# Expert routing by group, and the first two experts in passes by group

## The chip, the cores and the metric

The kernel runs on one core of one Trainium2 chip. The metric is the device time of one execution in microseconds. Before the change it is 599.27 us, the median of 3 runs (598.54 to 599.59).

## What is computed

The input is `x`, 16 batches of 128 rows of 256 float32 numbers (2048 tokens), and a context of the same shape. Four residual layers follow each other, each on the layer norm of `x`: a gated linear attention, a feed-forward layer with quantised weights and activations, a 16-head attention, and a mixture of experts. The change touches the last one, whose core in the reference is

```python
router_probs = jax.nn.softmax(router_logits, axis=-1)
gate, idx = jax.lax.top_k(router_probs, K)                 # K = 2 of 8 experts
mask_kt = jnp.swapaxes(mask, 1, 2).reshape(G, K * T, E)
pos = jnp.cumsum(mask_kt, axis=1) * mask_kt - 1.0          # place in the expert, within the group
disp_k = jax.nn.one_hot(pos, C, dtype=jnp.float32) * mask[..., None]
expert_in = jnp.einsum('gtec,gth->egch', dispatch, x)
h = jax.nn.relu(jnp.einsum('egch,ehf->egcf', expert_in, wi))
expert_out = jnp.einsum('egcf,efh->egch', h, wo)
y = jnp.einsum('gtec,egch->gth', combine, expert_out)
```

The tokens form G = 2 groups of T = 1024 (batches 0 to 7, and 8 to 15). Each expert takes at most C = 160 tokens of a group: 320 places in all. The place of a token depends on the tokens ahead of it in its own group only.

## The kernel before

The work is tiled by batch, 128 rows at a time ("tile" 0 to 15). The order on every engine is written out by hand, in one Python block per engine, and engines wait for each other on named semaphores (`pe.wait_ge(s["h_relu"], n)`). PE does the matmuls, VectorE (`dve`) and ScalarE (`act`) evacuate PSUM and do the elementwise work, POOL issues indirect DMAs (gathers and scatters of rows by index), SyncE (`sp`) the plain ones.

The end of the attention. VectorE and ScalarE normalise the tiles into `XR` (`norm4`, `norm4_act`); PE turns them two tiles at a time (`d_turn(p)`), ScalarE keeps the turned ones in `KT` (`xt4(p)`). PE computes the router's logits: tiles 0 to 7 in `d_logits`, 8 to 11 in `d_logits4`, both turned back by `d_back` and `d_back4`, and 12 to 15 by `d_row`. SyncE stores `XR` to the DRAM buffer `token_rows`, 4 tiles in a DMA.

The routing (L1386 to L1436, VectorE). When the logits of all tiles are there, the two largest of 8 are found for every token, one-hot in `OHs`; a scan gives the sums over tiles (`cum`); PE counts with two matmuls (L1989, L1991); `place` is each token's place in each expert. The softmax goes to `LG` and is stored as 8 more columns of each row in `token_rows`.

From places to token numbers, once for each expert e: `select(e)` (L1442) makes 16 one-hot matrices of 128 x 192 in `SEL`, one for each tile (for e = 0 ScalarE makes the last four, L871). PE multiplies them with the token numbers, split in two digits (`e_tokens`, L2004), VectorE keeps the result (`digits`, L1449), PE adds the digits up (`e_places`, L2013 to L2015), VectorE writes `token` (L1452). The 320 places are three chunks: chunk 0 and chunk 1 are the first 128 places of group 0 and of group 1, chunk 2 the last 32 places of both (64).

An expert. POOL gathers the three chunks of rows from `token_rows` into `XE` (`rows_in`, L511); VectorE takes the gate's column out (`gcol`, L1463); PE turns the rows (`e_turn`, L2041), ScalarE keeps them (`xet`, L888). `e_hidden`: 8 tiles of hidden units, each 2 float32 matmuls of 320 columns (L2057; a float32 matmul is two instructions in the trace), and a relu on ScalarE after each (`relu`, L895). `e_out`: chunk 2 (L2068), then chunk 0 (L2075), then the transposes of the next expert's rows, then chunk 1 (L2075). POOL gathers the running sums of the same tokens from `out` into `YG`, VectorE adds gate times result (`add_rows`, L1470 to L1478), POOL scatters the rows back (L513). The sums of an expert are gathered only after the scatter of the expert before has landed. The token and place matmuls of expert e + 1 stand inside `e_hidden(e)`, at hidden tiles 1 and 3 (4 and 6 for e = 0).

SyncE loads the 1 MB `wi` and `wo` of expert e + 2 as soon as expert e has left its buffer:

```python
free_after(sp, s["h_done"], e, NFT)     # wi: behind the last hidden matmul of e - 2
free_after(sp, s["ec_done"], e, 3)      # wo: behind the last output chunk of e - 2
```

Ahead of the rows of expert 0 PE runs dummy matmuls (`keep_busy`, L1498), 13 + 4 + 2 of them, two instructions each.

Of the kernel before, what the change touches and what calls it, by code (L numbers as in the profile page):

```python
# [7 lines left out]
BF16 = mybir.dt.bfloat16  # L8
# [77 lines left out]
def build(nc, A, out):  # L86
# [22 lines left out]
    with ctx:  # L109
# [218 lines left out]
        SEL_DVE = 12  # L328
# [16 lines left out]
        def _(sp):  # L345
# [38 lines left out]
            def weights_in(e, u, h):  # L384
                if isinstance(e, int) and e < 2:
                    sp.wait_ge(s["u_again"], len(LATE))
                free_after(sp, s["h_done"], e, NFT)
                sp.dma_start(WI[:, u], A["L1_ffn_wi"][bass.ds(e, 1)].squeeze(0).rearrange("(k p) f -> p k f", p=P)).then_inc(s[f"wi_in{u}"], 16)

            def weights_out(e, u, h):  # L390
                free_after(sp, s["ec_done"], e, 3)
                sp.dma_start(WO[:, u], A["L1_ffn_wo"][bass.ds(e, 1)].squeeze(0).rearrange("(k p) f -> p k f", p=P)).then_inc(s[f"wo_in{u}"], 16)
            weights_in(0, 0, 0)
            weights_out(0, 0, 0)
            weights_in(1, 1, 0)
            weights_out(1, 1, 0)

# [4 lines left out]
            xr = xr_d.rearrange("(b p) d -> p b d", p=P)  # L402
            for q in range(XQ):

                if q == 1:
                    sp.wait_ge(s["xr_act"], 4)
                else:
                    sp.wait_ge(s["xr_ready"], (2, 0, 4, 6)[q])
                sp.dma_start(xr[:, 4 * q:4 * q + 4, 0:D], XR[:, 4 * q:4 * q + 4, 0:D]).then_inc(s["xr_out"], 16)
            sp.wait_ge(s["probs"], 1)  # L410
            sp.dma_start(xr[:, :, D:], LG[:, :, :]).then_inc(s["xr_out"], 16)

            def both(e, u, h):
                if isinstance(e, int) and e < 2:
                    return
                weights_in(e, u, h)
                weights_out(e, u, h)
            steps(sp, NE, [(both, 0)])
# [5 lines left out]
        def _(pool):  # L424
# [77 lines left out]
            pool.wait_ge(s["xr_ready"], 6)  # L502
# [4 lines left out]
            def indirect(e, c, dram, sbuf, gather):  # L507
                n = P if c < 2 else ROWS - 2 * P
                where = bass.IndirectOffsetOnAxis(ap=token[0:n, e, c:c + 1], axis=0)
                if gather:  # L510
                    return nc.gpsimd.indirect_dma_start(out=sbuf[0:n, c, :], out_offset=None, in_=dram, in_offset=where,  # L511
                                                        bounds_check=NB * S - 1, oob_is_err=False)
                return nc.gpsimd.indirect_dma_start(out=dram, out_offset=where, in_=sbuf[0:n, c, :], in_offset=None,  # L513
                                                    bounds_check=NB * S - 1, oob_is_err=False)
            pool.wait_ge(s["xr_out"], 16 * (XQ + 1))
            pool.wait_ge(s["x3_out"], 16 * XQ)
            def rows_in(e):
                pool.wait_ge(s["token_ready"], e + 1)
                if e >= 2:
                    pool.wait_ge(s["xe_tr"], e - 1)  # L520
                    pool.wait_ge(s["gcol_ready"], e - 1)
                for c in range(3):

                    indirect(e, c, xr_d, XE[:, e % 2], True).then_inc(s[f"xe_in{e % 2}" if e or c == 2 else f"xe_first{c}"], 16)
            rows_in(0)
            for e in range(NE):
                if e + 1 < NE:
                    rows_in(e + 1)
                if e >= 1:
                    pool.wait_ge(s["rows_out"], 16 * 3 * e)  # L530
                for c in range(3):
                    indirect(e, c, out_rows, YG, True).then_inc(s["yg_in"], 16)
                for n, c in enumerate((2, 0, 1)):
                    pool.wait_ge(s["y_ready"], 3 * e + n + 1)
                    indirect(e, c, out_rows, YG, False).then_inc(s["rows_out"], 16)
# [3 lines left out]
        def _(act):  # L539
# [257 lines left out]
            def lt4_copy():  # L797
                act.wait_ge(s["d_lg"], 2)
                nc.scalar.activation(XCT[:, 1, 0, :], ps[7][:, 0:P], ACT.Copy).then_inc(s["d_lt"], 1)
# [54 lines left out]
            xt4(0)  # L854
            xt4(1)
# [1250 lines left out]
```

## Time and profile before

| | |
|---|---|
| median of 3 runs | 599.27 us |
| the profiled execution | 599.31 us, its span 597.6 us |
| PE busy | 515.6 us (86% of the span) |
| VectorE, ScalarE, POOL busy | 375.3, 321.8, 141.2 us |
| first hidden matmul of expert 0 | 431.67 us |
| first hidden matmul of expert 2 | 472.47 us |
| moved by DMA | 37.58 MB |

All times in what follows count from the start of the span, in the one profiled execution; the time of a run is the span and 1.7 us around it. A row of a timeline gives start, duration, engine, line, what was written from what, the shapes, a count where rows are merged, and in brackets how long the engine was idle before and what ended that. The chain of waits is the path that ended last, followed back from the end.

### The profile page before, as it was taken

To read this page: it belongs to the slowest core of one execution; us is meant where nothing else is said; L and a number is where in the kernel's file an instruction comes from. 1 tells how busy PE (TensorE), PEld (TensorE's weight loads), DVE (VectorE), ACT (ScalarE), POOL (GpSimd) and SP (SyncE) were. 2 spreads that over 40 slices of the span, in tenths; PEclk is the share of its full clock that TensorE was granted. 3 is DMA by queue.
4 is the path that set the end of the run, shared out by engine and by line. 5 is a ranking of instruction groups with operands and counts; after the bars stand their busy time and mean duration, and the time that the engine had idled before them with its cause. 6 is when DMAs were issued, how large, how long until landed. Compare 5 with 4: busy or idle time off the path is not lost.

```text
span 597.6 us, 9312 instructions
## 1 busy us (share of the span) xinstructions
PE 515.6 (86%) x3284; PEld 364.1 (61%) x3284; DVE 375.3 (63%) x944; ACT 321.8 (54%) x672; POOL 141.2 (24%) x202
## 2 busy tenths in 40 slices
PE   1979989899999700899989999996799999999994
PEld 1558846654444300787657787874667776777773
DVE  6576689845489989779678699987403332143101
ACT  1836658723389969771298899984222112211220
POOL 2005635000000000000323133111234344434431
PEclk9979999999999955999999999999699999999998
DMA  7910000000000000025000101015133536353410
GB/s 213 274 53 1 2 2 1 2 1 0 0 0 1 0 1 1 0 102 181 2 0 2 36 3 37 1 38 176 28 110 120 185 120 204 118 183 120 133 44 22
DMA packets 31994, 37.58 MB, mean 63 GB/s; under 512 B 8656, under 2 KB 27728, under 8 KB 31952
## 3 DMA queue, kind: packets, MB, share of 16 engines
q1 hardware_dynamic: 28880, 29.07, 14.8%
q0 software_dynamic: 3072, 7.95, 4.6%
q8 instruction: 26, 0.43, 0.3%
q14 instruction: 16, 0.13, 0.1%
HBM read 30.14 MB, written 6.88 MB: 62 GB/s over the span
## 4 chain that ended last, share of the span: by engine, by line
PE 71%; DVE 14%; ACT 8%; issue 2%; SPq 2%; DMA 1%; POOL 1%; POOLq 0%; DVEq 0%
PE pA L2057 12%; PE pB L2075 9%; PE pC L1726 6%; PE pC L1765 5%; PE pA L1759 3%; PE pB L1775 3%; PE pA L1681 2%; PE pC L1587 2%; PE pC L1681 2%; PE pB L1681 2%; PE pC L2068 2%; DVE am L1180 2%; PE pC L1633 2%; PE pB L1855 2%; DVE arena L1176 2%
## 5 line engine op out<-in xcount | busy, mean ns | idle before, releaser
L477 POOL TENSOR_TENSOR arena<-KT,par 128x256 f32<-128x256 f32 x32 | 19.0, 614 | 248.0 <-DVE XIT L1254 186.0
L2057 PE MATMUL pA<-arena 128*128 128x320 f32 x256 | 74.1, 438 | 0.4 <-ACT arena L883 0.4
L895 ACT ACTIVATE arena<-pA 128x320 f32<-128x320 f32 x64 | 28.0, 437 | 71.8 <-PE pA L2057 71.8
L2075 PE MATMUL pB<-arena 128*128 128x256 f32 x256 | 59.3, 385 | 0.0
L2057 PEld LDWEIGHTS pA<-arena 128*128 128x128 f32 x256 | 47.4, 190 | 18.9 <-issue 1.1
L2075 PEld LDWEIGHTS pB<-arena 128*128 128x128 f32 x256 | 47.4, 190 | 9.4 <-issue 3.1
L1146 DVE TENSOR_REDUCE am<-arena 128x1 f32<-128x512 f32 x48 | 32.1, 681 | 23.0 <-ACT arena L647 22.9
L1726 PE MATMUL pC<-wdnT,XIT 128*128 128x256 f32 x192 | 42.9, 381 | 1.8 <-DVE XIT L1254 1.8
L1330 DVE TENSOR_REDUCE rm<-pA 128x16 f32<-128x2048 f32 x16 | 36.7, 2291 | 8.8 <-PE pA L1759 8.8
L1726 PEld LDWEIGHTS pC<-wdnT,XIT 128*128 128x128 f32 x192 | 36.0, 190 | 7.9 <-DVE XIT L1254 2.8
L1765 PE MATMUL pC<-ident,arena 128*128 128x128 f32 x240 | 35.4, 280 | 1.5 <-ACT XIT L743 0.8
L513 POOL DMA_INDIRECT out<-arena,token x24 | 23.5, 977 | 55.1 <-DVE arena L1478 45.7
L780 ACT ACTIVATE arena<-pC 128x512 f32<-128x512 f32 x60 | 34.9, 605 | 0.9 <-PE pC L1765 0.9
L511 POOL DMA_INDIRECT arena<-token_rows,token x24 | 24.2, 1010 | 44.3 <-DVE token L1452 26.2
L1463 DVE COPY gcol<-arena 128x3 f32<-128x3 f32 x8 | 1.4, 174 | 52.8 <-DMA arena<-token_rows,token 52.8
L1765 PEld LDWEIGHTS pC<-ident,arena 128*128 128x128 f32 x240 | 26.1, 141 | 10.4 <-ACT arena L767 4.6
L1498 PE MATMUL pB<-ident 128*128 128x128 f32 x64 | 12.5, 372 | 21.7 <-DVE arena L1227 21.7
L1339 DVE TENSOR_TENSOR arena<-pA,rm 128x1024 f32<-128x1024 f32 (+1 forms) x32 | 29.1, 952 | 0.5
L888 ACT ACTIVATE arena<-pA 128x320 f32<-128x320 f32 x14 | 5.4, 435 | 43.8 <-PE pA L2041 43.8
L767 ACT ACTIVATE arena<-arena 128x1024 f32<-128x1024 f32 (+1 forms) x32 | 28.1, 881 | 0.0
L511 POOL DMA_INDIRECT arena<-out,token x24 | 23.7, 988 | 9.2 <-issue 7.0
L1498 PEld LDWEIGHTS pB<-ident 128*128 128x128 f32 x64 | 11.7, 280 | 21.8 <-issue 21.7
(341 smaller groups left out, 1152.7 us busy)
## 6 DMA issues: line engine op xcount, KB each, us to landing
arena<-in_L_ffn_wi SPq DMA_DIRECT2D x8, 1024.0 KB, 5.3
arena<-in_L_ffn_wo SPq DMA_DIRECT2D x8, 1024.0 KB, 5.8
X<-in_x SPq DMA_DIRECT2D x4, 512.0 KB, 6.3
arena<-in_ctx SPq DMA_DIRECT2D x4, 512.0 KB, 7.8
out<-X SPq DMA_DIRECT2D x4, 512.0 KB, 2.9
token_rows<-arena SPq DMA_DIRECT2D x4, 512.0 KB, 5.4
arena<-in_L_ffn_w_up SPq DMA_DIRECT2D x1, 768.0 KB, 7.8
arena<-in_L_ffn_w_gate SPq DMA_DIRECT2D x1, 768.0 KB, 9.7
```

The lines of the kernel that those rows point to most:

```text
L511: return nc.gpsimd.indirect_dma_start(out=sbuf[0:n, c, :], out_offset=None, in_=dram, in_offset=where, bounds_check=NB * S - 1, oob_is_err ...
L767: nc.scalar.activation(part, part, ACT.Exp).then_inc(s["p_ready"], 1)
L780: nc.scalar.activation(PT[:, u, 4 * g:4 * g + 4, :], bank.rearrange("p (k n) -> p k n", k=4), ACT.Copy).then_inc(s["pt_ready"], 1)
L895: nc.scalar.activation(HT[:, u, f, :], ps[2 + f % 2][:, 0:ROWS], ACT.Relu).then_inc(s["h_relu"], 1)
L1146: V_.tensor_reduce(am[:, 0 if name == "gate" else 1, cols(c * FT + f, 1)], t[:, f, cols(c, 512)], AX.X, ALU.max, apply_absolute_value=True ...
L1330: V_.tensor_reduce(rm[:, u, :], sco, AX.X, ALU.max, negate=True).then_inc(s["rm_ready"], 1)
L1339: V_.tensor_tensor(PR[:, u, part], sco[:, part], rm[:, u, part].unsqueeze(2).broadcast_to([P, part.stop - part.start, P]), ALU.add).then_i ...
L1681: last = mm(ps[2 + f][:, :], w[:, k, f * P:(f + 1) * P], XITv[:, k, cols(c, 512)], start=(k == 0), stop=(k == KD - 1))
L1726: last = mm(ps[6 + u][:, 0:D], OT[:, u, f, :], wdnT[:, f, :], start=(f == 0), stop=(f == FT - 1))
L1765: last = tr(bank[:, n * P:(n + 1) * P], PR[:, u, 4 * g + n, :], ident[:, :])
L2057: last = mm(ps[2 + f % 2][:, 0:ROWS], WI[:, u, k, f * P:(f + 1) * P], XET[:, u, k, :], start=(k == 0), stop=(k == KD - 1))
L2075: last = mm(ps[4 + c][:, 0:D], HT[:, u, f, c * P:(c + 1) * P], WO[:, u, f, :], start=(f == 0), stop=(f == NFT - 1))
```

## The change

Everything of the routing that depends on one group is done for that group alone. Group 0 goes first, as soon as the logits of tiles 0 to 7 are there. Expert 0 and expert 1 are done in two passes each, in the order (0, A), (1, A), (0, B), (1, B): pass A is chunk 0 (128 places, all of group 0), pass B the other 192 places. Experts 2 to 7 are one pass "F" each, as before. The routing of group 1 stands on VectorE between the steps of passes 0 and 1.

```diff
-        SEL_DVE = 12
+        PASSES = [(0, "A"), (1, "A"), (0, "B"), (1, "B")] + [(e, "F") for e in range(2, NE)]
+        CHUNKS = {"A": (0,), "B": (2, 1), "F": (2, 0, 1)}
+        GROUPS = {"A": (0,), "B": (1,), "F": (0, 1)}
```

SyncE: the rows and probabilities of each group have a semaphore of their own, and `wi` and `wo` wait for the passes:

```diff
+            def normed_out(q):
+
+                if q % 2:
+                    sp.wait_ge(s["xr_act"], 2 * q + 2)
+                else:
+                    sp.wait_ge(s["xr_ready"], q + 2)
+                sp.dma_start(xr[:, 4 * q:4 * q + 4, 0:D], XR[:, 4 * q:4 * q + 4, 0:D]).then_inc(s[f"xr_out{q // 2}"], 16)
...
             for q in range(XQ):
...
+                normed_out(q)
+            probs_out(0)
+            probs_out(1)
+            for e in range(2, NE):
+                weights_in(e, e % 2)
+                weights_out(e, e % 2)
```

POOL: the gathers of the A passes start when group 0 is in `token_rows`:

```diff
+            pool.wait_ge(s["xr_out0"], 16 * 3)
+            rows_in(0)
+            rows_in(1)
             pool.wait_ge(s["x3_out"], 16 * XQ)
...
+            sums_in(0)
+            pool.wait_ge(s["xr_out1"], 16 * 3)
+            rows_in(2)
+            sums_out(0)
+            rows_in(3)
+            for i in range(1, len(PASSES)):
+                if 3 <= i < len(PASSES) - 1:
+                    rows_in(i + 1)
+                sums_in(i)
+                sums_out(i)
```

ScalarE: the turned tiles 0 to 3 are kept ahead of the last `at_copy`, the logits' copy goes ahead of the last inverse square root, and the normalisation of tiles 12 to 15 comes from VectorE. The four selections on ScalarE are gone (VectorE makes them).

```diff
             at_copy(NB - 2, 1 - u)
+            xt4(0)
+            xt4(1)
             at_copy(NB - 1, u)
...
             xt4(3)
+            lt_copy()
             rsqrt(8, 4, 12)
             xt4(4)
             xt4(5)
-            lt_copy()
             lt4_copy()
+            act.wait_ge(s["xr_ready"], 5)
+            for b in range(12, NB):
+                norm4_act(b)
+            exp4(0)
             xt4(6)
             xt4(7)
...
+            exp4(1)
```

VectorE: the same steps as before, for one group of 8 tiles at a time:

```diff
+            logits_0()
+            largest(0)
+            less_largest(0)
+            link(choose(0, 0))
+            chosen_off(0)
+            second(0)
+            tile_sums(0)
+            probabilities(0)
+            find_places(0)
+            select(0, 0)
+            logits_1()
+            digits_kept(0)
+            largest(1)
+            less_largest(1)
+            number(0)
+
+            select(1, 0)
+            link(choose(1, 0))
+            chosen_off(1)
+            digits_kept(1)
+            second(1)
+            number(1)
+            tile_sums(1)
+            probabilities(1)
+            find_places(1)
+            select(0, 1)
+            gate_column(0)
+            digits_kept(2)
+            select(1, 1)
+            number(2)
+            add_rows(0)
+            digits_kept(3)
+            gate_column(1)
+            number(3)
+            for i in range(2, len(PASSES)):
+                if i >= 4:
+                    digits_kept(i)
+                    number(i)
+                gate_column(i)
+                if i == 2 or 4 <= i < len(PASSES) - 1:
+                    for g in range(NG):
+                        select(2 if i == 2 else i - 1, g)
+                add_rows(i - 1)
+            add_rows(len(PASSES) - 1)
```

PE: the places inside the passes, and the start. The transposes of the next pass stand ahead of the last full chunk, in an A pass inside its only chunk:

```diff
+            def e_hidden(i):
...
+                    if i == 0 and f == 2:
+                        count(1)
+                    if i == 1 and f == 2:
+                        e_tokens(3)
+                    if i == 1 and f == 5:
+                        e_places(3)
+                    if 3 <= i < len(PASSES) - 1 and f == 1:
+                        e_tokens(i + 1)
+                    if 3 <= i < len(PASSES) - 1 and f == 3:
+                        e_places(i + 1)
...
+                for c in full:
+                    if c == full[-1] and part != "A" and i + 1 < len(PASSES):
+
+                        e_turn(i + 1)
+                    for f in range(NFT):
+                        if part == "A":
+                            if i == 0 and f == 1:
+                                e_tokens(2)
+                            if (i, f) in ((0, 4), (1, 6)):
+                                e_turn(i + 1)
+                            if i == 0 and f == 5:
+                                e_places(2)
...
             d_turn(6)
-            d_back()
-            d_back4()
             d_turn(7)
+            count(0)
             for b in range(12, NB):
                 d_row(b)
...
             e_tokens(0)
             e_places(0)
-            e_turn(0, 0, 0)
-            flat(NE, [(e_hidden, 0), (e_out, 0)])
+            keep_busy(ps[4], 8)
+            e_tokens(1)
+            e_places(1)
+            keep_busy(ps[4], 8)
+            e_turn(0)
+            for i in range(len(PASSES)):
+                e_hidden(i)
+                e_out(i)
```

The order of the indirect DMAs on POOL, from the first one on. Before (`token_rows` are gathers of rows, `out` as a source gathers of sums, `out` as a target scatters; each row is a chunk, or as many as its count says):

```order
L511 DMA arena<-token_rows,token 128x264 x2
L511 DMA arena<-token_rows,token 64x264
L511 DMA arena<-token_rows,token 128x264 x2
L511 DMA arena<-token_rows,token 64x264
L511 DMA arena<-out,token 128x256 x2
L511 DMA arena<-out,token 64x256
L513 DMA out<-arena,token 2048x256 x3
```

and now:

```order
L530 DMA arena<-token_rows,token 128x264 x2
L530 DMA arena<-out,token 128x256
L530 DMA arena<-token_rows,token 128x264
L530 DMA arena<-token_rows,token 64x264
L532 DMA out<-arena,token 2048x256
L530 DMA arena<-token_rows,token 128x264
L530 DMA arena<-token_rows,token 64x264
L530 DMA arena<-out,token 128x256
L532 DMA out<-arena,token 2048x256
L530 DMA arena<-out,token 128x256
L530 DMA arena<-out,token 64x256
L532 DMA out<-arena,token 2048x256 x2
```

One chunk of rows, not three, stands ahead of the first pass; the next three rows of expert 2 (L530, `token_rows`) follow behind the last row shown, the two scatters of pass 2.

PE at the end of an expert and the start of the next, before:

```order
L2068 MATMUL pC<-arena 64x256 x8
L2075 MATMUL pB<-arena 128x256 x8
L2041 MATMUL pA<-ident,arena 128x128 x2
L2041 MATMUL pA<-ident,arena 128x64
L2041 MATMUL pA<-ident,arena 128x128 x2
L2041 MATMUL pA<-ident,arena 128x64
L2075 MATMUL pB<-arena 128x256 x8
L2057 MATMUL pA<-arena 128x320 x2
```

and now, at the end of pass 3 (expert 1, B), ahead of expert 2:

```order
L2141 MATMUL pA<-arena 128x192 x10
L2155 MATMUL pC<-arena 64x256 x8
L2118 MATMUL pA<-ident,arena 128x128 x2
L2118 MATMUL pA<-ident,arena 128x64
L2118 MATMUL pA<-ident,arena 128x128 x2
L2118 MATMUL pA<-ident,arena 128x64
L2171 MATMUL pB<-arena 128x256 x8
L2141 MATMUL pA<-arena 128x320 x2
```

One full chunk of 8 matmuls less stands between the hidden part and the transposes of expert 2's rows.

## Rows read from the trace of the kernel before

**Rows 1.** The page: granted clock of TensorE in 40 slices, and the weight loads of the hidden matmuls.
```profile
PEclk9979999999999955999999999999699999999998
...
L2057 PEld LDWEIGHTS pA<-arena 128*128 128x128 f32 x256 | 47.4, 190 | 18.9 <-issue 1.1
```

**Rows 2.** Windows: span, its length, busy us and count of each engine, granted clock, DMA.
```profile
410.00:420.00 10.00, 2.94 (x22) 2.27 (x20) 7.73 (x30) 2.15 (x7) 1.33 (x2) 0.78 0.42 116
420.00:430.00 10.00, 8.49 (x55) 7.53 (x56) 1.77 (x9) 1.76 (x5) 3.23 (x3) 0.54 0.16 37
```

**Rows 3.** The chain of waits, 395 to 600 us: start, us, what.
```profile
423.27 5.84 PE pB L1498 x26
429.11 0.37 PE pA L2025 x2
429.48 0.89 PE pB L1498 x8
...
431.67 4.57 PE pA L2057 x16
...
442.85 4.90 DMA arena<-token_rows,token
...
462.30 1.88 PE pC L2068 x16
464.18 3.65 PE pB L2075 x16
467.82 0.99 PE pA L2041 x6
...
472.47 1.08 PE pA L2057 x4
473.55 0.44 PE pC L2004 x16
...
571.50 8.61 PE pA L2057 x32
```

**Rows 4.** Timeline of VectorE, 397 to 500 us: start, us, instructions, idle before.
```profile
407.00 0.16 DVE L927 TENSOR_TENSOR s<-yv 128x4 f32<-128x4 f32 x1 [0.67 <-ACT yv L546]
...
409.90 0.23 DVE L1390 COPY XIT<-pB 128x64 f32<-128x64 f32 x1 [0.73 <-PE pB L1899]
...
412.26 0.19 DVE L1397 COPY XIT<-pC 128x32 f32<-128x32 f32 x1 [1.48 <-PE pC L1909]
...
418.76 2.24 DVE L1442 TENSOR_SCALAR arena<-cidx,XIT 128x192 bf16<-128x192 bf16 x12
422.25 0.56 DVE L1449 CAST XIT<-pC 128x384 bf16<-128x384 f32 x1 [1.25 <-PE pC L2004]
423.31 0.22 DVE L1452 TENSOR_SCALAR token<-pC 128x2 uint32<-128x2 f32 x2 [0.50 <-PE pC L2015]
...
463.02 0.20 DVE L1463 COPY gcol<-arena 128x3 f32<-128x3 f32 x1 [6.05 <-DMA arena<-token_rows,token]
...
468.44 0.43 DVE L1470 COPY arena<-pC 64x256 f32<-64x256 f32 x1 [2.36 <-DMA arena<-out,token]
```

**Rows 5.** Timeline of ScalarE, 397 to 432 us: the normalisation of two tiles.
```profile
399.78 1.12 ACT L791 ACTIVATE arena<-X,s,rstd 128x256 f32<-128x256 f32 x2
```

**Rows 6.** Timeline of POOL, 425 to 500 us, and of SyncE's queue: DMA issues.
```profile
424.54 1.27 POOL L511 DMA_INDIRECT arena<-token_rows,token  x1 [13.21 <-issue]
...
440.25 1.00 POOL L511 DMA_INDIRECT arena<-token_rows,token  x1 [11.86 <-DVE token L1452]
...
457.79 1.05 POOL L511 DMA_INDIRECT arena<-token_rows,token  x1 [1.13 <-DVE token L1452]
...
464.32 0.97 POOL L511 DMA_INDIRECT arena<-out,token  x1 [0.30 <-issue]
...
441.76 0.39 SPq L388 DMA_DIRECT2D arena<-in_L_ffn_wi  x1
```

**Rows 7.** The chain of waits, 46 to 60 us: matmuls of 128 float32 columns.
```profile
51.80 1.98 PE pC L1587 x16
```

More of the change, by code:

```diff
@@ L516, in _, with rows_in @@
-            pool.wait_ge(s["x3_out"], 16 * XQ)
[L517 to L535, printed above, removed]
+            def rows_in(i):
+                e, part = PASSES[i]
+                pool.wait_ge(s["token_ready"], i + 1)
+                if part == "F":
+                    pool.wait_ge(s["xe_tr"], i - 1)
+                    pool.wait_ge(s["gcol_ready"], i - 1)
+                for c in sorted(CHUNKS[part]):
+                    indirect(e, c, xr_d[0:TG * S, :] if part == "A" else xr_d, XE[:, e % 2], True, (TG if part == "A" else NB) * S).then_inc(s[arrived(i)[0]], 16)
@@ L896, in _, with relu @@
-            steps(act, NE, [(xet, 0), (relu, 0)])
+            def relu(i):
+                e, part = PASSES[i]
+                if part == "F":
+                    act.wait_ge(s["ec_done"], PIECES[i - 1])
+                n = places(part)
+                for f in range(NFT):
+                    act.wait_ge(s["h_done"], i * NFT + f + 1)
+                    nc.scalar.activation(HT[:, e % 2, f, n], ps[2 + f % 2][:, 0:n.stop - n.start], ACT.Relu).then_inc(s["h_relu"], 1)
+            for i in range(len(PASSES)):
+                xet(i)
+                relu(i)
@@ new lines, in select, with digits_kept @@
+            def select(e, g):
+                if e >= 2 and g == 0:
+                    dve.wait_ge(s["id_done"], e + 1)
+                for b in range(g * TG, (g + 1) * TG):
+                    last = V_.tensor_scalar(SEL[:, e % 2, b, :], cidx[:, g, :], place[:, g, e, b % TG:b % TG + 1], None, ALU.is_equal)
+                last.then_inc(s["sel_ready"], 1)
+            def digits_kept(i):
+                e, part = PASSES[i]
+                n = slice(SELW * GROUPS[part][0], SELW * (GROUPS[part][-1] + 1))
+                dve.wait_ge(s["id_done"], i + 1)
+                V_.tensor_copy(digits[:, e % 2, n], ps[7][:, n]).then_inc(s["id_kept"], 1)
@@ new lines, in e_tokens @@
+            def e_tokens(i):
+                e, part = PASSES[i]
+                if i >= 1:
+                    pe.wait_ge(s["token_ready"], i)
+                for g in GROUPS[part]:
+                    pe.wait_ge(s["sel_ready"], i + 1 if i < 4 else 2 * e + g + 1)
+                    for b in range(g * TG, (g + 1) * TG):
+                        o = 32 * (b % 4)
+                        last = mm(ps[7][o:o + 32, g * SELW:(g + 1) * SELW], ids[:, 2 * b:2 * b + 32], SEL[:, e % 2, b, :],
+                                  start=(b % TG < 4), stop=(b % TG >= 4))
+                last.then_inc(s["id_done"], 1)
@@ new lines, in e_turn @@
+            def e_turn(i):
+                e, part = PASSES[i]
+                u = e % 2
+                name, n = arrived(i)
+                pe.wait_ge(s[name], n)
+                if i >= 1:
+                    pe.wait_ge(s["xet_ready"], i)
+                for k in range(KD):
+                    for c in sorted(CHUNKS[part]):
+                        n = P if c < 2 else SHORT
+                        if part == "A":
+                            last = tr(ps[u][:, k * P:(k + 1) * P], XE[:, u, 0, k * P:(k + 1) * P], ident[:, :])
+                        else:
+                            o = c * P - places(part).start
+                            last = tr(ps[k][:, o:o + n], XE[0:n, u, c, k * P:(k + 1) * P], ident[0:n, 0:n])
+                last.then_inc(s["xe_tr"], 1)
```

402 lines of the change are left out of this document (176 added, 226 removed).

## The prediction

> **What bounds the kernel now.** I first read the page: the TensorE clock is full in most slices, but two stretches and a few single slices stand below [rows 1]. The diff touches only the end of attention and the expert stage, so I then read the windows around 400 to 480 us. From 410 to 420 us PE works 2.9 of 10 us, and from 420 to 430 us it works 8.5 us at a granted clock of 0.54 [rows 2]. The chain of waits says what that work is: 5.84 us of 26 dummy matmuls (L1498) that only keep the array busy until the rows of expert 0 arrive, and the first useful expert matmul is at 431.67 us [rows 3]. From there PE is the chain: an expert costs 19.8 us, 8.6 of them hidden matmuls (L2057), 1.88 the short chunk (L2068), 3.65 each full chunk (L2075), 0.99 the transposes, 0.44 the token matmuls of the next expert (L2004). So two things set the end: when the experts start, and how long PE takes from there. Between 412 and 424 us the chain is VectorE, one small instruction after another [rows 4].
>
> **The change, part by part.** Times are absolute, in the profiled execution (span 597.6 us, 599.31 us in all; the median of the runs is 599.27, so the two agree).
>
> *Group 0 is routed first.* Before, the whole routing starts when the last logits are there, at 412.26 us, and ends with the tokens at 423.31 + 0.22 = 423.53 [rows 4]. Now the chain of group 0 needs only tiles 0 to 7. I follow it: four evacuated transposes, the logits, their copy and the transpose back end near 408.35 us; VectorE then still has its inverse square root, which waits for ScalarE as before (407.00, [rows 4]), but behind the 0.6 us copy of the logits that now goes ahead of it, so about 409.0. Four normalisations that stood ahead of the logits copy went to ScalarE, 0.56 each [rows 5], 2.2 us beside VectorE's chain. The logits take 0.5 us. The 17 linked steps to the places are 64 wide instead of 128. A 64-wide copy takes 0.23 [rows 4], a step with its issue 0.26 to 0.28, so 4.7 us. Eight selections cost 8 x 2.24/12 = 1.5 us; then come logits of group 1 (0.4), the digits at half width (0.35 instead of 0.56), two steps of group 1 (0.5), and the places and the number (0.2). That gives tokens at 417.2 us, **6.3 us earlier**.
>
> *One gather instead of three ahead of the first matmul.* Before it was 431.67 - 423.53 = 8.1 us. Now: POOL starts its DMA 1.0 us after the tokens, and the first gather was down 429.11 - 424.54 = 4.6 us later, by the transposes that follow it [rows 3, 6]; then come 4 transposes' instructions (0.11 each, from L1498 at full clock, 8 in 0.89 [rows 3]), 0.2 of drain and one 0.4 us copy: 6.5 us, **1.6 us less**. The dummy matmuls (two blocks of 16 instructions, 1.8 us each at full clock) are hidden by that landing if the clock stays up. First expert matmul: 423.7 us, **8.0 us earlier**.
>
> *Two experts become four passes.* Before, experts 0 and 1 take 472.47 - 431.67 = 40.8 us [rows 3]. The columns are the same, but narrow matmuls are not as cheap as their width. For 128 columns the trace has a row of the same kind, L1587: 16 instructions in 1.98 us, 0.124 each [rows 7], where 320 columns cost 8.61/32 = 0.269 [rows 3]. Each hidden tile of pass A has 4 of them, 0.50 us, and must wait for the relu of two tiles before: 0.50 + some 0.35 of drain and signals + 0.28 for the relu make 1.13 us per two tiles, 4.5 us in all. In pass B, 192 columns give 0.16 each, 5.3 us.
> Pass 0: 4.5 + 0.2 (counting of group 1) + 3.65 + 0.2 (tokens) + 0.45 (transposes) + 0.1 (places) = 9.1. Pass 1: 4.5 + 0.3 + 3.65 + 0.65 = 9.1. Pass 2: 5.3 + 1.9 + 0.65 + 3.65 = 11.5. Pass 3: 5.3 + 0.45 + 0.2 + 0.45 (waits for the digits, which stand behind the additions of pass 2 on VectorE) + 1.9 + 1.0 + 3.65 = 12.95. Sum 42.65: **1.85 us more**, without waits for rows.
> The bounds of the unknown price of 128 columns: 0.107, the width alone scaled from 320 columns, and 0.190, the duration of a weight load of L2057 [rows 1], if loads can't overlap. L1587 loads 128x128 float32 weights too and repeats at 0.124, so I take that. The Trainium skill ("TensorE: Matmul & The Clock Gate", LDWEIGHTS) says that a load takes columns / 1.2 ns whatever the matmul's width; its 107 ns for 128 columns would make a pass A's hidden part 3.4 us at best. This is no end of my range.
>
> *A new wait, at the end of pass 3.* Expert 2's rows are transposed after the short chunk and **one** full chunk before (5.5 us after the hidden part); in pass 3 the order is short chunk, transposes, full chunk, so only 1.9 us after. Let T be the start of pass 3's hidden part. PE wants the rows at T + 6.4 + 1.9 = T + 8.3. POOL has queued ahead of them the two stores of pass 2, and those wait for the additions, which wait for sums gathered at about T - 5 and T - 3.7 (sums land 4.1 us after the last issue, 464.32 to 468.44 in the steady stage [rows 4, 6]); so the additions end at T + 2.2, the stores at T + 4.8, and the three gathers start at T + 5.1. A quiet gather of three takes 463.02 - 457.79 = 5.2 us [rows 4, 6]; but SP loads the 1 MB of `wi` of expert 3 when the hidden part ends, at T + 6.4, 1.3 us behind the first gather. Expert 1 of before has the same collision: gathers from 440.25, `wi` at 441.76, rows at 447.75, 7.5 us [rows 3, 6]. That is 7.5 us after the first gather and 6.0 after `wi`. So the rows come at T + 12.4 to 12.6, and PE waits **4.0 us** or a little more; quiet it is 2.0, and with the sums there in time and quiet, 1.0. I take 4.0, since the offset of `wi` is nearest to the row of expert 1.
> The Trainium skill ("DMA: Bandwidth & Descriptors", Anatomy of one DMA) gives a transfer issued by GpSimd 2.0 us fixed plus its bytes; by it the last gather would land about T + 11, and the wait would be 2.7. The rows of before, 5.2 and 7.5 for three, are above it.
>
> *What costs nothing.* Group 1's routing (some 7 us of VectorE up to 430 us) stands beside passes 0 and 1, 18 us in which VectorE has little else; if it slipped past them, pass 2 would wait for its rows, needed at about 440 and landed by about 438. The probabilities of group 0 are stored in a queue behind the last quarter of the rows, at 413.7, and are there by 417.1; POOL needs them at 418.2. The number of indirect DMAs stays 72, and the tail is the same.
>
> Sum: -8.0 + 1.85 + 4.0 = -2.15, so 599.31 - 2.15 = **597.2 us**.
>
> **The rivals.**
> 1. *Small collision.* The wait in pass 3 is 1.0 to 2.5 us: 594.2 to 595.7. For it: in the steady stage gathers land in 5.2 us. Against it: the load of `wi` begins beside them.
> 2. *The clock falls in the routing* (slower). Before, it fell after PE's work stopped at 412 us and came back only at 429 us, after the long dummy block, whose instructions took 0.225 each in it [rows 2, 3]. Now PE has short bursts in 410 to 422 us (transposes, logits, tokens, dummies) with gaps of 0.5 to 1.8 us. If these don't hold the clock, the single-tile logits (1.8 us more, 1.3 behind VectorE), the dummies (3.6 us per block, the second now ending after the rows are there) and the transposes bring the first expert matmul to about 427.2, 3.5 us later, and the hidden part may run slowly for up to 3 us, 1.5 more: 600.7 to 602.2. It decides wherever the clock falls between 410 and 422 us. Against it: no gap is as long as the one of before.
> 3. *Narrow matmuls are bound by weight loads of 0.19.* Hidden parts of 32 x 0.19 = 6.1 us in four passes: 2 x 1.6 + 2 x 0.8 = 4.8 more, and the wait in pass 3 gives nothing back, since it goes with T: 602.0. Against it stands L1587 at 0.124.
> 4. *The overlap is not reached*, since group 1's rows are late for pass 2. Every us there is one us; 2 us make 599.2.
>
> **How the numbers follow.** Forecast 0.5, small collision 0.17, clock 0.2, weight loads 0.04, late group 1 0.09. A measurement can tell about 0.2%, 1.2 us. The forecast itself has +-1.5 us from its steps, so a fifth of it lies within 1.2 us of no change; faster is 0.40 + 0.17 + 0.04 (half of late group 1) = 0.61, the same 0.10 + 0.04 = 0.14, slower 0.20 + 0.04 + 0.01 = 0.25. The range goes from the small collision with its lower bounds, 593.0 (the width alone at 128 columns takes another 1.0 off), into the clock's case, 601.0, and leaves out about 2 in 10.
>
> **What would show it.** In the profile after: first hidden matmul near 423.7 us; passes of 9, 9, 11.5 and 17 us; 32 hidden matmuls of 128 columns in about 4.5 us; a DMA wait of PE near 461 us of some 4 us in front of expert 2's transposes, and the experts from 2 on 19.8 us each. A granted clock of 0.5 between 412 and 425 us, or a wait ahead of pass 2, would prove it wrong.

## The result and the profile after

| | before | after |
|---|---|---|
| median | 599.17 us (598.52 to 599.59, 5 runs) | 602.48 us (601.61 to 603.18, 5 runs) |
| span of the profiled execution | 597.6 us | 600.6 us |
| first hidden matmul | 431.67 | 425.54 |
| first hidden matmul of expert 2 | 472.47 | 475.46 |
| mean granted clock over the span | 0.948 | 0.946 |

The ratio is 1.005, 95% interval 1.0039 to 1.0062: slower by half a per cent, outside the range given. The experts do start 6.1 us earlier, but the four passes to expert 2 take 9.1 us more than the two experts did.

The page's clock line of after (40 slices of 15.0 us) has two dips behind 400 us where the one of before has one [rows 1]: a 7 from 405 to 420 us, earlier than the 6 of before, and a new 7 from 465 to 480 us.
```profile
PEclk9979999999999955999999999997999799999998
```

The windows of after: length, busy us (count) of PE, PE weight load, VectorE, ScalarE, POOL, then granted clock, DMA share, GB/s. The first two answer to [rows 2].
```profile
410.00:420.00 10.00, 8.09 (x49) 7.11 (x46) 7.81 (x39) 3.72 (x9) 0.60 (x1) 0.63 0.40 119
420.00:430.00 10.00, 8.99 (x72) 7.88 (x70) 5.55 (x26) 2.36 (x9) 2.68 (x3) 0.86 0.23 45
460.00:470.00 10.00, 5.86 (x34) 3.77 (x33) 2.32 (x14) 1.39 (x6) 4.37 (x5) 0.86 0.57 180
470.00:480.00 10.00, 10.00 (x50) 7.36 (x50) 3.29 (x11) 1.71 (x5) 1.94 (x2) 0.80 0.34 108
```
From 410 to 420 us PE is busy for 8.1 us where it was busy for 2.9, and still the granted clock is 0.63, below the 0.78 of before. Part of the 8.1 us is the same work stretched by the half clock, so a busy share says little of how much work was done. In the trace the granted clock stands at 0.5 (the level of 1.2 GHz) from 412.6 to 422.8 us and from 467.2 to 474.0 us.

The chain of waits of after, at the start: start, us, what. It answers to [rows 3].
```profile
413.68 3.32 PE pC L1994 x16
417.00 0.47 PE pC L2088 x7
...
418.16 3.62 PE pB L1585 x16
421.78 0.47 PE pC L2088 x7
...
422.95 1.90 PE pB L1585 x16
424.84 0.23 PE pA L2115 x2
...
425.54 1.16 PE pA L2141 x8
...
426.80 3.12 PE pA L2141 x24
```
The clock can be read from the durations: the same block of 16 dummy instructions (L1585) took 3.62 us the first time and 1.90 the second, once ahead of the clock's return at 422.8 us and once behind it. The sixteen logits instructions of the last four tiles (L1994) took 3.32 us at half clock.

The timeline of VectorE of after (idle before and its releaser in brackets) shows who paid for that; it answers to [rows 4].
```profile
414.30 1.53 DVE L1488 TENSOR_SCALAR arena<-cidx,XIT 128x192 bf16<-128x192 bf16 x8
417.10 0.19 DVE L1436 COPY XIT<-pC 128x32 f32<-128x32 f32 x1 [1.27 <-PE pC L1994]
...
418.22 0.15 DVE L1501 TENSOR_SCALAR token<-pC 128x1 uint32<-128x1 f32 x1
```
VectorE was at the selections on time (414.30, forecast 414.2), then waited 1.27 us for logits that PE still had in hand. The tokens are there at 418.37 instead of the forecast 417.2.

The second place is the end of pass 3, in PE's timeline of after:
```profile
461.62 1.95 PE L2155 MATMUL pC<-arena 128*64 128x256 f32 x16
467.70 1.90 PE L2118 MATMUL pA<-ident,arena 128*128 128x128 f32 x6 [4.14 <-DMA arena<-token_rows,token]
469.53 5.93 PE L2171 MATMUL pB<-arena 128*128 128x256 f32 x16
475.29 1.24 PE L2141 MATMUL pA<-arena 128*128 128x320 f32 x4
```
The wait for expert 2's rows is 4.14 us. Behind it the six transposes take 1.90 us where [rows 3] have 0.99, and the full chunk 5.86 in the chain (5.93 here, with its drain) where [rows 3] have 3.65: 0.9 + 2.2 = 3.1 us that are no wait at all and stand in no idle column.

Why the rows were late shows in the queues of POOL and SyncE (SPq) of after:
```profile
458.08 1.01 POOL L532 DMA_INDIRECT out<-arena,token  x1 [0.30 <-issue]
459.40 1.03 POOL L530 DMA_INDIRECT arena<-token_rows,token  x1 [0.31 <-issue]
460.74 1.02 POOL L530 DMA_INDIRECT arena<-token_rows,token  x1 [0.30 <-issue]
462.07 0.95 POOL L530 DMA_INDIRECT arena<-token_rows,token  x1 [0.30 <-issue]
...
461.72 0.37 SPq L404 DMA_DIRECT2D arena<-in_L_ffn_wi  x1
```
The last gather was issued at 462.07, the load of `wi` at 461.72, and the rows were down at 467.66, 5.59 us after the issue. The chain of waits of after shows what stood in line before them:
```profile
441.15 2.80 DMA arena<-out,token
...
445.28 2.45 DMA out<-arena,token
...
449.86 4.74 DMA arena<-out,token
...
462.07 5.59 DMA arena<-token_rows,token
```
From 437.5 to 467.7 us this chain runs through POOL, the transfers and VectorE's additions, and not through PE: sums of pass 1, its store, sums of pass 2, its stores, and only then the rows of expert 2. PE does its passes beside that and then waits for its end. So the wait can be shortened by a faster transfer (e2 below) or by another order on POOL (e4).

### The profile page after: what moved, and what is told of

The parts are those of the page before. It is cut to its first block, busy times and chain, and to the rows that moved or that the text cites. A ratio compares the mean times of both kernels' runs of the same rounds, so it can differ in the third digit from the quotient of the medians.

```text
span 600.6 us, 9381 instructions
## 1 busy us (share of the span) xinstructions
PE 521.1 (87%) x3344; PEld 372.4 (62%) x3344; DVE 377.8 (63%) x968; ACT 323.5 (54%) x687; POOL 141.5 (24%) x202
## 4 chain that ended last, share of the span: by engine, by line
PE 69%; DVE 13%; ACT 8%; DMA 4%; issue 3%; POOL 1%; POOLq 0%; SPq 0%; DVEq 0%
PE pA L2141 10%; PE pB L2171 9%; PE pC L1813 6%; PE pC L1852 5%; PE pA L1846 3%; PE pB L1862 3%; PE pA L1768 2%; PE pC L1674 2%; PE pB L1768 2%; PE pC L1768 2%; DVE am L1217 2%; PE pC L1720 2%; PE pB L1942 2%; DVE arena L1213 2%; DVE am L1183 2%
## 5 line engine op out<-in xcount | busy, mean ns | idle before, releaser
L2141 PE MATMUL pA<-arena 128*128 128x320 f32 (+2 forms) x320 | 75.8, 387 | 0.5 <-ACT arena L916 0.5
L930 ACT ACTIVATE arena<-pA 128x320 f32<-128x320 f32 (+2 forms) x80 | 30.7, 384 | 75.6 <-PE pA L2141 75.6
L2141 PEld LDWEIGHTS pA<-arena 128*128 128x128 f32 x320 | 53.8, 190 | 15.9 <-issue 0.9
L2171 PE MATMUL pB<-arena 128*128 128x256 f32 x256 | 62.2, 396 | 0.0
L2171 PEld LDWEIGHTS pB<-arena 128*128 128x128 f32 x256 | 48.7, 196 | 9.3 <-issue 2.5
L530 POOL DMA_INDIRECT arena<-token_rows,token x24 | 24.4, 1015 | 44.4 <-DVE token L1501 25.3
L1585 PE MATMUL pB<-ident 128*128 128x128 f32 x58 | 10.7, 359 | 21.7 <-DVE arena L1264 21.7
L920 ACT ACTIVATE arena<-pA 128x320 f32<-128x320 f32 (+1 forms) x16 | 5.7, 408 | 43.6 <-PE pA L2118 43.6
L1511 DVE COPY gcol<-arena 128x3 f32<-128x3 f32 (+2 forms) x10 | 1.6, 164 | 40.1 <-DMA arena<-token_rows,token 40.1
L530 POOL DMA_INDIRECT arena<-out,token x24 | 23.8, 991 | 11.2 <-issue 6.7
L1521 DVE COPY arena<-pC 64x256 f32<-64x256 f32 x8 | 3.4, 426 | 33.7 <-DMA arena<-out,token 23.6
```

Of the source, the lines that this page charges most:

```text
L930: nc.scalar.activation(HT[:, e % 2, f, n], ps[2 + f % 2][:, 0:n.stop - n.start], ACT.Relu).then_inc(s["h_relu"], 1)
L2141: last = mm(ps[2 + f % 2][:, 0:n.stop - n.start], WI[:, u, k, f * P:(f + 1) * P], XET[:, u, k, n], start=(k == 0), stop=(k == KD - 1))
L2171: last = mm(ps[4 + c][:, 0:D], HT[:, u, f, c * P:(c + 1) * P], WO[:, u, f, :], start=(f == 0), stop=(f == NFT - 1))
```

## The experiments

Theory A: the prediction's three terms hold, and what it left out is the clock, which fell in the routing (1.8 us at the start) and again in the new wait (3.1 us behind it). Theory B: the pieces after the wait are slow for another reason (the transfers beside them, the split itself), and only a shorter chain helps. All ratios are to the kernel before on the same chip.

### Fill the wait (e1_warm_wait)

```diff
+                        if i == 3:
+                            pe.wait_ge(s["xet_ready"], 4)
+                            keep_busy(ps[0], 17)
                         e_turn(i + 1)
```

> The changed kernel (602.5 us) with 17 dummy matmuls (34 instructions, 0.11 us each, 3.8 us) ahead of the transposes of expert 2's rows, in the 4.1 us that PE waits there. Theory A: the wait itself costs 4.1 us, and the clock that falls in it another 3.1 us (transposes 1.9 for 1.0, the full chunk behind them 5.86 for 3.65). Then the wait stays, the clock stays at 1.00, and the time is 602.5 - 3.1 = 599.4. Theory B: the slow instructions behind the wait are slow for another reason (the 1 MB load beside them): 602.5, with the chunk at 5.9 us at a full clock.

Measured: 600.01 us (599.07 to 602.35, 10 runs), ratio 1.0022 (1.0008 to 1.0036); span 597.3, 3.3 less. PE's timeline, end of pass 3:
```profile
463.50 4.06 PE L1585 MATMUL pA<-ident 128*128 128x128 f32 x34
467.39 1.16 PE L2118 MATMUL pA<-ident,arena 128*128 128x128 f32 x6
468.48 3.72 PE L2174 MATMUL pB<-arena 128*128 128x256 f32 x16
```
The rows come only about half a us earlier (VectorE's copy of their gate column, which waits for them, starts at 467.13 instead of 467.68), but the transposes and the chunk run at full speed behind the dummies. Of the 3.3 us in the span 0.2 are an earlier first hidden matmul (425.30). This is the cleanest proof in the case: nothing was taken away, work of no use was added, and the kernel became 2.5 us faster in the medians, 1.7 by the two ratios (1.005 and 1.0022, whose intervals don't touch).

### Take the load out of the wait (e2_wi_late)

```diff
+                if e == 3:
+                    sp.wait_ge(s["xe_in0"], 16 * 5)
                 sp.dma_start(WI[:, u], A["L1_ffn_wi"][bass.ds(e, 1)]...
```

> The changed kernel with the load of wi of expert 3 held back on SyncE's queue until expert 2's rows have landed. Theory A: this load is what makes the three gathers take 8.3 us instead of the 5.2 of a quiet stage; rows at 459.4 + 5.2 = 464.6, PE wants them at 463.5, so a wait of 1.1 instead of 4.1, too short for the clock to fall: 602.5 - 3.0 - 3.1 = 596.4. Theory B: the gathers are late because of what is ahead of them on POOL or because of the stores of pass 2 that are still under way: landing stays at 467.7, 602.5.

Measured: 596.37 us (596.01 to 597.13, 4 runs), ratio 0.9956 (0.994 to 0.9973). POOL and SyncE:
```profile
461.63 0.95 POOL L532 DMA_INDIRECT arena<-token_rows,token  x1 [0.30 <-issue]
...
464.27 0.37 SPq L406 DMA_DIRECT2D arena<-in_L_ffn_wi  x1
```
the last gather's landing in the chain of waits:
```profile
461.63 2.33 DMA arena<-token_rows,token
```
and PE:
```profile
464.24 1.21 PE L2120 MATMUL pA<-ident,arena 128*128 128x128 f32 x6 [1.01 <-DMA arena<-token_rows,token]
465.38 3.72 PE L2173 MATMUL pB<-arena 128*128 128x256 f32 x16
```
With the 1 MB load behind it instead of beside it, the transposes can start 2.6 us after the last gather's issue instead of 5.6. The wait is 1.01 us, and no clock falls behind it. One wait on SyncE turns the change from slower into faster than before.

### Transposes later in the last chunk (e3_turn_late)

The transposes of expert 2's rows go behind six of the chunk's eight tiles in pass 3; the transfers are not touched.

> The changed kernel, with the transposes of expert 2's rows inside the last full chunk of pass 3, ahead of its 7th tile, not ahead of the chunk: PE wants the rows 2.75 us later, at 466.3, for a landing at 467.7. Theory A: a wait of 1.4 us, clock at 1.00: 602.5 - 2.7 - 3.1 = 596.7, if ScalarE's copy of the turned rows (0.8 us) hides behind the last two tiles. Theory B (clock or no clock, what stands behind is slow): 599.8.

Measured: 598.09 us (595.86 to 600.98, 10 runs), ratio 0.9978 (0.9958 to 0.9998). The wait was 1.23 us, and the granted clock from 460 to 480 us was 1.00, as expected. The median came out 1.4 us above the expectation; the profiled run stood 1.7 us late from before 402 us on, ahead of anything that was changed.

### Rows of expert 2 before the sums of pass 2 (e4_early_tokens)

The tokens of expert 2 are found in pass 2 (not 3), and POOL gathers its rows ahead of pass 2's sums and stores:

```diff
             for i in range(1, len(PASSES)):
-                if 3 <= i < len(PASSES) - 1:
+                if i == 2:
+                    rows_in(4)
+                if 4 <= i < len(PASSES) - 1:
                     rows_in(i + 1)
```

> The changed kernel, with the tokens of expert 2 found in pass 2 (not pass 3) and its rows gathered ahead of the sums of pass 2. Theory A: the rows are there by about 455, PE never waits for them: 602.5 - 4.1 - 3.1 = 595.3. The sums of pass 2 are gathered 2.6 us later, additions end at 459, ahead of the output of pass 3 at 461.6, so nothing is given back. Rival: POOL's queue is what bounds the stage, the additions of pass 2 come after 461.6 and PE waits for them instead: 597 to 599.

Measured: 596.60 us (595.42 to 597.09, 4 runs), ratio 0.995 (0.9933 to 0.9966). No wait is left in pass 3, and expert 2 starts at 470.08 instead of 475.46. At the start the clock was low for 13.7 us in this execution (10.2 in after), and the first hidden matmul was at 426.99: these 1.45 us are about the 1.3 that the expectation missed.

### Are the dummy blocks worth their time? (e6_no_dummies, e7_one_block)

On e4's order, `keep_busy(ps[4], 8)` is taken out at both places (e6), or replaced by one block of 12 just ahead of the transposes (e7).

> The kernel of e4 (596.6 us) without the two blocks of 8 dummy matmuls ahead of the first expert matmul. Theory A: the first hidden matmul is held back by the second block at half clock, not by the rows, which are there at about 424; without the blocks it comes at 424.8, but then passes 0 and 1 start at half clock, the hidden part of pass 0 takes 7 us for 4.3 and more behind it until the clock is back: 2 us earlier and 4 to 7 us slower, 598.5 to 601.5. Theory B: real matmuls bring the clock back as fast as dummies do, and the blocks are only in the way: 595.

> The kernel of e4 (596.6 us) without the first block of 8 dummies, and 12 instead of 8 in the second. At half clock the first block takes 3.6 us, in which the tokens of expert 1 wait behind it; without it the tokens of expert 1 come 1.7 us earlier and the one block of 24 instructions runs from about 421 to 426 at half clock, at best rising in between: the same first hidden matmul, 596.6 +- 0.8, if the clock rises after a stretch of full work of the same length; 595 if it rises earlier since the work is in one piece.

Measured: e6 596.34 us (595.87 to 597.5, 6 runs), ratio 0.9956 (0.9938 to 0.9973); e7 597.53 us (596.37 to 599.42, 12 runs), ratio 0.9972 (0.9959 to 0.9985). Neither is measurably apart from e4. PE's timeline of e6:
```profile
424.33 2.07 PE L2147 MATMUL pA<-arena 128*128 128x128 f32 x8 [0.47 <-ACT arena L918]
...
426.41 4.11 PE L2147 MATMUL pA<-arena 128*128 128x128 f32 x24
```
Without the blocks the first pass starts 2.7 us before e4's and runs its hidden part at half clock, 6.0 us instead of 4.3; with them the clock is back in time, but the second block, stretched to 3.7 us by the half clock, stands in the way. In the profiled executions e6 keeps 1.1 us of its lead (pass 2 begins at 444.05, in e4 at 445.18), in the medians 0.3 us are left, within the noise. Once the clock has fallen, dummies only buy back what they cost.

### Keep the clock from falling: dummies in the gaps (e5_warm_start, e8_warm_after)

```diff
             d_turn(5)
+            pe.wait_ge(s["x3_ready"], NB)
+            keep_busy(ps[5], 3)
             d_logits4()
+            keep_busy(ps[5], 2)
             d_back4()
+            keep_busy(ps[5], 3)
...
             d_turn(6)
+            keep_busy(ps[5], 1)
             d_turn(7)
```

The same lines on e4's order (e5) and on the changed kernel itself (e8).

> The kernel of e4 (596.6 us) with 9 dummy matmuls (18 instructions) in the gaps in which PE waits between 408.6 and 412.4 us, that is before the place at which the clock fell in all five profiles so far. Theory A: the clock falls because PE had too little to do in those gaps; filled, it stays at 1.00, the single-tile logits take 1.8 us for 3.5, the dummy blocks 1.8 for 3.6 and the first hidden matmul comes at 423.6, not 426.5 to 427.0: 596.6 - 3 = 593.6. Theory B: the clock falls anyway, because what PE does around 413 to 418 us is too thin too (8 columns per matmul), somewhat later: 595 to 597.

> The changed kernel itself (602.5 us) with the same dummies in the gaps between 408.6 and 412.4 us as e5. It tells the clock at the start from the wait in pass 3. Theory A: 1.9 us earlier start, the wait of 4.1 us and the clock that falls in it as before: 602.5 - 1.9 = 600.6, if the clock holds. Theory B: it falls all the same: 602.5.

Measured: e8 600.87 us (599.8 to 603.54, 12 runs), ratio 1.0031 (1.0016 to 1.0047): 1.6 us less than after in the medians (the intervals of the two ratios overlap), with the clock low for 3.4 us only and the first hidden matmul at 424.10; the wait in pass 3 and the fall behind it stayed. e5 602.08 us (599.33 to 605.33, 10 runs), ratio 1.0047 (1.0026 to 1.0068): 5.5 us slower than e4, against both expectations, though its start was 1.1 us earlier than e4's. Its chain of waits shows a new one:
```profile
460.44 1.00 POOL out L532
461.44 0.30 issue
461.75 5.85 DMA out<-arena,token
...
468.41 1.03 POOL arena L530
469.44 0.30 issue
469.75 5.05 DMA arena<-out,token
...
477.13 0.21 PE pC L2107 x2
```
and PE's timeline what it did:
```profile
470.19 2.42 PE L2151 MATMUL pA<-arena 128*128 128x320 f32 x8
477.13 0.21 PE L2107 MATMUL pC<-pick,XIT 128*128 128x1 bf16 x2 [4.52 <-DVE XIT L1497]
...
477.48 7.89 PE L2151 MATMUL pA<-arena 128*128 128x320 f32 x18
```
The load of `wi` was now issued at 462.10, 0.35 us behind the last store of pass 2 (461.75), and the store took 5.85 us, where a store of after with no load beside it (pass 1, 445.28) has 2.45 in the chain. The sums of pass 3 wait for that store, their additions stand on VectorE ahead of the digits of expert 3 (L1497), and PE waits for its places 4.52 us; then the clock falls again (18 hidden instructions in 7.89 us, 0.44 each, where 0.28 is usual). In e6, which has the same order, `wi` came 0.98 us after the store (461.32, 462.30), POOL could go on to the sums 3.3 us after that store's issue (6.7 in e5), and no such wait is there. That is no more than the 3.3 us of e9 below, where the load was held back, so 0.98 us between store and load were enough. The same load, at the same place of the program, hit another transfer.

### Hold the load again, then fill the start (e9, e10, e11)

e9 is e5 with the load of expert 3's `wi` held until the stores of pass 2 are down:

```diff
+                if e == 3:
+                    sp.wait_ge(s["rows_out"], 16 * PIECES[3])
```

e10 is e9 with one dummy behind each single-tile step, and e11 is e10 without the two blocks of 8:

```diff
             for b in range(12, NB):
                 d_row(b)
+                keep_busy(ps[4], 1)
```

> The kernel of e5_warm_start (early tokens, dummies in the gaps at the start), with one thing more: SyncE issues the wi load of expert 3 only when the stores of pass 2 have landed. Theory A (in e5 the load of 1 MB that was issued 0.35 us after those stores made them land 6.7 us after their issue, for 3.3 in e6, so that the sums of pass 3 were late, TensorE waited 4.5 us for the places of expert 3, and its clock fell): the stores land at about 465.1, no wait of over 1 us at 477, no low clock after 430, and a time of 595.5. Theory B (the stores were late by chance or by the gathers in front of them on their queue): the wait and the fall stay, 601 to 602. If the load itself comes too late for expert 3 (it needs it at about 477 and the load takes some 6 us from 465): no cost expected.

> e9_hold_wi with one dummy matmul more after each single-tile step of the router's transposes, so that TensorE is busy also where it did 8-column matmuls with waits between them. Theory A (the clock falls at the start because TensorE is idle for much of 408 to 420): the clock stays at 1.00 through the routing, the first hidden matmul starts at about 423.6 and at full pace, 593.2. Theory B (it falls in the long wait for the tokens, whatever is done before): low for some 10 us as in e5, 595.5.

> e10_warm_rows without the two blocks of 8 dummies ahead of the experts. If the blocks only delay the first hidden matmul (as e6 against e4 said), it starts some 1 us earlier than in e10 but at half clock if the clock falls without them: 594 to 595.5. If they hold the clock, this is 1 to 3 us slower than e10.

| | us | ratio | first hidden matmul |
|---|---|---|---|
| e9 | 594.96 (592.98 to 596.47, 6 runs) | 0.9922 (0.9898 to 0.9947) | 424.55 |
| e10 | 593.48 (593.08 to 595.07, 6 runs) | 0.9903 (0.9884 to 0.9922) | 423.33 |
| e11 | 594.78 (594.53 to 596.41, 6 runs) | 0.9924 (0.9905 to 0.9943) | 422.58, at half clock |

e9 against e5 shows that the collision was e5's loss: the sums are gathered at 463.37 and 464.71 instead of 468.41 and 469.75, the wait for the places is gone, and 7.1 us of the median with it. In the two profiled executions the difference is 8.9 us: 1.4 are the start, where the clock was low for 3.4 us in e9 and 10.2 in e5, in spite of the same program up to there, and 7.5 lie behind it.

The clock line of e10's page and its windows:
```profile
PEclk9979998999999955899999999999999999999998
...
410.00:420.00 10.00, 8.73 (x92) 7.46 (x83) 8.72 (x44) 3.72 (x9) 1.27 (x1) 1.00 0.42 126
420.00:430.00 10.00, 8.96 (x72) 7.80 (x73) 6.20 (x31) 2.61 (x9) 2.01 (x2) 1.00 0.23 45
```
e11, windows:
```profile
410.00:420.00 10.00, 6.87 (x68) 5.71 (x64) 8.73 (x43) 3.72 (x9) 1.27 (x1) 0.91 0.40 118
420.00:430.00 10.00, 8.29 (x47) 7.37 (x47) 4.51 (x22) 2.60 (x9) 2.00 (x2) 0.57 0.24 45
```
In the profiled execution of e10 the granted clock does not fall in the routing nor behind it (only the last slice, past the last matmuls, is below 9), and the first hidden matmul is at 423.33, which is where the prediction had put it (423.7). In e11 it falls where the blocks are missing, and the first pass's hidden part is slow again; that is 1.3 us in the medians and 1.7 in the spans. The two intervals overlap, but both kernels ran on the same chip, and five of the six executions of e10 are below all six of e11. So the blocks that were worth nothing in e4 are worth more than a microsecond here: they hold a clock, they don't bring it back for free.

### The change's own order, clock held at both places (e12_clock_held)

The changed kernel, with e8's dummies, the one behind each `d_row`, and e1's 17 in the wait.

> The changed kernel with its order of instructions kept, and only dummy matmuls added at both places where the clock fell: 9 in the gaps and one after each single-tile step at the start (as in e10_warm_rows), and 17 in the wait for expert 2's rows (as in e1_warm_wait). Theory A (the prediction's sum was right apart from the clock: start of the passes -8, split +2, wait +4): the first hidden matmul at about 423.4, no granted clock of 0.5 between 400 us and the end of the matmuls, a wait of some 4 us in pass 3 filled with dummies, and 597.3 in all. Theory B (holding the clock at the start moves the fall or a transfer elsewhere, as in e5_warm_start): 600 or more.

Measured: 598.55 us (596.78 to 600.93, 12 runs), ratio 0.9997 (0.9984 to 1.0009). The profiled execution took 597.21 us (span 595.4):
```profile
423.02 1.16 PE L2145 MATMUL pA<-arena 128*128 128x128 f32 x8 [0.47 <-ACT arena L916]
```
and at the end of pass 3
```profile
461.19 4.10 PE L1585 MATMUL pA<-ident 128*128 128x128 f32 x34
465.43 1.21 PE L2122 MATMUL pA<-ident,arena 128*128 128x128 f32 x6
466.57 3.72 PE L2178 MATMUL pB<-arena 128*128 128x256 f32 x16
470.13 1.24 PE L2145 MATMUL pA<-arena 128*128 128x320 f32 x4
```
Its start is 8.65 us earlier than before's (423.02 for 431.67). Expert 2 begins at 470.29 in the chain of waits, so the passes take 47.3 us for 40.8, 6.5 more, and 6.5 - 8.65 = -2.2 us is the difference of the spans (595.4 and 597.6). That is the prediction's sum (-2.15) with the clock out of it.

The median is 1.3 us above that one execution, and the runs spread over 4 us. The mean granted clock of each execution tells a part of it. Six have 0.957 or more, as the profiled one (0.958), and a median of 597.4 us; the other six have 0.952 to 0.955 and a median of 599.1. By an estimate, 0.003 less over 595 us is 3.6 us more at half clock. That fits a clock that these dummies don't hold in every execution, but where the 3.6 us lie no trace shows. Two of the first six are slow all the same (599.13 and 600.93 us), and that stays open too. So the sum is shown on one execution and fits the median of six; over all twelve the change with these dummies is no faster than before.

## Why the prediction was wrong

| step of the prediction | forecast | measured |
|---|---|---|
| selections start on VectorE | 414.2 | 414.30 |
| tokens of group 0 | 417.2 | 418.37 |
| first hidden matmul | 423.7 | 425.54 |
| passes 0, 1, 2 | 9.1, 9.1, 11.5 | 8.9, 9.0, 11.8 |
| pass 3 without wait or clock | 12.95 | 20.2 - 4.1 - 3.1 = 13.0 |
| wait for expert 2's rows | 4.0 | 4.14 |
| half clock behind that wait | not in the sum | 3.1 |
| all | -2.15 | -6.1 + 1.9 + 4.1 + 3.1 = +3.0 |

**The failed step** is the one on the new wait. Its size was right to 0.14 us, but it was priced as a wait alone. The prediction had put the fall of the clock into the routing only, as a rival, and never asked what the clock does in the gap that it forecast itself; it cost 3.1 us, half of the 6.3 us for which the clock stayed low behind the wait (467.7 to 474.0). e1, which fills the wait, has the transposes and the chunk back at full speed. The kernel before had the same collision at expert 1, but a full chunk of 3.65 us covered it, and PE idled 0.70 us there, which is why no row of before showed the price.

That the size of the wait came out so well is part luck. The gathers started 4.2 us after the hidden part of pass 3 did, not 5.1, and took 8.3 us and not 7.5; the two errors cancel. What held is the time from the load of `wi` to the rows: 5.9 us, forecast 6.0 from expert 1 of before.

**The start** was mis-sized by 1.8 us, because the clock fell there as well. That is the prediction's second rival, which had 0.20. Its steps were the right ones (slow logits, VectorE 1.3 us late for them, slow dummies), only its sum was too large (427.2 for 425.54), since the clock was back at 422.8 and the second block and the hidden part ran at full speed. The argument against it, "no gap is as long as the one of before", was the wrong one: the clock fell at 412.6, after the bursts and gaps of 0.3 to 0.7 us between 408.8 and 412.5. With those gaps filled the fall comes later (417.3 us in e8), and with dummies among the single-tile logits too it is gone from the profiled executions of e10 and e12.
With neither fall the sum stands in e12's profiled execution (597.21), with 0.65 us more gained at the start than forecast and as much more spent in the passes. With both it is -2.15 + 1.8 + 3.1 = +2.8, where the spans show +3.0.

**What was right.** The order of VectorE's chain, the price of a narrow matmul (24 instructions in 3.12 us, 0.130 each, forecast 0.124 by [rows 7], with the relu's pace 4.3 us for a hidden part against 4.5), the four passes together to 0.1 us without the wait and the clock (each by itself to 0.3), group 1 beside the passes (its rows were down at 437.9 us, before PE wanted them), and the collision with `wi`.
On that collision the prediction weighed the Trainium skill ("DMA: Bandwidth & Descriptors", Anatomy of one DMA), whose 2.0 us fixed plus bytes would have given, as an estimate, a wait of 2.7. The traces have 2.6 us from the last gather's issue to the transposes in e2, with the load held back, and 5.6 in after, with the load beside it. The page's figure is near the quiet case and says nothing of the crowded one, and here the crowded one decides.
The Trainium skill ("TensorE: Matmul & The Clock Gate", HAM oscillation) tells of a kernel whose DMA waits let the clock fall, so that what follows each wait starts slowly. Pass 3 of after is such a place: 4.14 us idle, then 7.8 us for what takes 4.6. The prediction did not draw on it where it was needed.

## What to carry to other kernels

A forecast wait of several us on TensorE has two prices: the wait, and the instructions behind it at half clock; here 4.1 and 3.1 us. Dummies are worth having ahead of a fall (e10) and next to nothing after it (e6), so look for the first gap, not for the slow stretch.
When work moves, list the large loads that start on an engine's progress, and ask which indirect transfer each will now start beside: one wait on SyncE was worth 6 to 7 us, in e2 as in e9, and the same load hit the gathers in one order and the stores in the other. The best kernel here, e10, has the change, the rows early, the load held and the clock held, and is faster than before by 1.0% (ratio 0.9884 to 0.9922).

## What the runs showed of the hardware

- The clock can fall although TensorE is busy most of the time: in after it fell at 412.6 us, behind idle gaps of 0.3 to 0.7 us only. In e5, with those gaps filled, it fell later, at 414.9 us, near the end of the sixteen 8-column logits instructions (413.08 to 415.07) and not in the gaps ahead of them. In e10 and e12, with dummies among these, it did not fall in the profiled execution. Which property of the 8-column stretch counts was not tested.
- The same program up to that point had the clock low for 10.2 us in e5 and 3.4 us in e9. A fall is not the same in each execution. The executions of e5 and e12 spread over 4 to 6 us, those of e10 over 2; that the fall is what spreads them is not shown.
- A 1 MB load that starts within 0.4 us of an indirect transfer more than doubled the time of that transfer: from the last gather's issue to the rows 5.59 us beside it (after) and 2.33 without (e2), a store 5.85 beside it (e5) and 2.45 without (after, pass 1). A load 0.98 us behind the store's issue cost nothing (e6: 3.3 us until POOL went on, as in e9 with the load held).
